# Graph kernel: late weight chunks held back and reordered, gathered source rows issued 12 tiles ahead, logits split on ScalarE

## The chip, the cores and the metric

The kernel runs on one core of one Trainium2 chip. The metric is device time in microseconds (us) of one execution; a profile shows a single execution's engines, queues and waits. Engines are named as in the profile: PE is TensorE's matmuls and PEld its weight loads, DVE is VectorE, ACT is ScalarE, POOL is GpSimd, SP is SyncE, which only issues transfers here.

## What is computed

256 nodes with 1024 features and 8448 edges (src, dst), sorted by dst.

```python
h = relu(layernorm(x))
feat = concat([h[src], h[dst]], 1)                    # 8448 x 2048
e_f = relu(feat @ W_kind + b_kind)                    # kind: hh (128 edges), oo (640), ho (the rest)
logit = (e_f @ W_a + b_a)[:, 0]
alpha = softmax of logit over the edges of each dst
z = segment_sum(alpha * h[src], dst)                  # 256 x 1024
x = x + relu(concat([h, z], 1) @ W_hn (rows 0 to 63) or W_on (the others) + b)
h = relu(layernorm(x))
x = x + h @ Wd.T + bias                               # Wd: 1024 edge weights scattered; here by 256 x 256 counts
```

## The kernel before, in words

The edges lie in 66 tiles of 128. For the oo and ho edges the product with `W_kind` is taken per node and not per edge: TensorE makes the tables P = h @ top half and Q = h @ bottom half, ScalarE stores them in HBM, and POOL gathers a tile's P rows by src into `Gp` (12 slots, `p_rows`, L308) and its Q rows by dst into `Gq` (8 slots, `q_rows`, L320), 512 KB each. The first tile (hh, tile number 0 in the code) goes through TensorE directly.

`lots()` cuts the 66 tiles into 24 lots of mostly 3. The 65 gathered tiles are counted 0 to 64 below in the order of `GATHERED`; lot 2 is the hh tile, lots 17 and 18 are oo, lot 19 holds gathered tiles 53 to 55, lot 20 56 to 58, lot 21 59 to 61, lot 22 62 and 63, lot 23 64.

- VectorE, per tile: `total` (L584) adds P and Q rows and counts `s_sum`; `onehot` (L575, L577) makes the one-hot maps of src and dst for the next lot; `logit` (L588) takes relu times `wa` with a row sum and counts `s_used`. Per lot: `lot_split` (L630, L631) adds b_a and cuts the logits into a high part `lgh` and a rest `lgl`. It stands behind the first sum of the next lot (`lot_start`). After lot 19 comes `few_max`, after lot 20 `few_sums`.
- ScalarE, per tile: the source one-hots times edge weights (`weight_products`, L414, high and low) and, when the split is through, times logits (`logit_products`, L426, high and low).
- TensorE, per lot g: first `JOBS_IN[g]` jobs, then `lot_count(g + 1)` (L809 into psB and psW), then `lot_place(g)` (L809 into psA, 12 matmuls for 3 tiles). `PACE` lists the jobs of lots 3 on. A job of the first three units is one chunk of 512 KB (L897, 16 matmuls); the last unit has eight jobs, 0 to 7, each with a pair of chunks "on" and "hn" of the top halves (L914, L919, L921). Jobs 0 and 1 stand in lot 16, jobs 2 to 5 in lots 17 to 20, and jobs 6 and 7 behind the last placing. Then come the transposes of A (L941), the products with `rows_h` (L950) and the lower halves (L955, L975, L980).
- SP loads weight chunks into the 4 slots of `W` (L227), each as soon as the job four chunks (in the last unit two jobs) before has used the slot. Behind the last of these stand, in this order, eight hn chunks (L247) and `rows_h` (L250), which go into slots of `Gp` as their last tiles are used, the last bias (L252), and x again (L254 to L257).
- POOL issues 12 P gathers, 12 Q gathers, and then Q and P of each tile in turn. Q(i) waits for the sum of tile i - 8, P(i) for the logit of tile i - 12.

After the last lot VectorE makes the softmax (L674 to L700), whose result A the transposes wait for.

The last job and its loads in `block.sync`, which say what the order is:

```python
for q in range(WSLOTS, CHUNKS):
    ...
    sp.wait_ge(s_wused, uses_before(q))
    load(q)
for k in range(KC):
    sp.wait_ge(s_used, FREED + k + 1)
    sp.dma_start(hn_w[k], ...).then_inc(s_hn, 16)
```

Here FREED is 53.

Of the kernel before, what the change touches and what calls it, by code (L numbers as in the profile page):

```python
# [4 lines left out]
P = 128  # L5
N = 256
NT = N // P
D = 1024
KC = D // P
# [8 lines left out]
LOT = 3  # L18
# [12 lines left out]
LOTS = lots()  # L31
# [4 lines left out]
ENTRY = [len(EARLY) + sum(map(len, LOTS[:g])) for g in range(NLOTS + 1)]  # L36
# [6 lines left out]
WSLOTS = 4  # L43
NP = 12
NQ = 8
# [7 lines left out]
CHUNKS = SPLIT + HH + PLAIN + 2 * KC  # L53
PACE = [2, 2, 2, 2] + [2, 2, 1, 2, 1] + [2, 2, 2, 2] + [2, 1, 1, 1, 1]
# [3 lines left out]
HN_SLOT = [(FREED + k) % NP for k in range(KC)]  # L58
ROW_SLOT = (FREED + KC) % NP
# [10 lines left out]
FREED_Q = len(GATHERED) - NQ  # L70
assert FREED_Q % NQ + 3 <= NQ
# [3 lines left out]
def uses_before(q):  # L75

    gone = q - WSLOTS
    return gone + 1 if gone < SPLIT + HH + PLAIN else SPLIT + HH + PLAIN + (gone - SPLIT - HH - PLAIN) // 2 + 1


def gnn_block(nc, x, edge_ids, edge_w, weights, bias_rows, w_a, b_a, l1_bias, out):
# [13 lines left out]
    with ctx:  # L95
# [59 lines left out]
        lgl = sb("lgl", [P, 2, LOT], f32r)  # L155
# [43 lines left out]
        s_hh, s_split = sem("hh_logit"), sem("logits_split")  # L199
# [22 lines left out]
        def _(sp):  # L222
# [14 lines left out]
            for q in range(WSLOTS, CHUNKS):  # L237
                if q - WSLOTS < SPLIT:
                    sp.wait_ge(s_lo, q - WSLOTS + 1)
                else:  # L240
                    sp.wait_ge(s_wused, uses_before(q))
                load(q)
                if q == 2 * WSLOTS:
                    sp.dma_start(wa[:, :], w_a.broadcast_to((P, D))).then_inc(s_wa, 16)
            for k in range(KC):
                sp.wait_ge(s_used, FREED + k + 1)
                sp.dma_start(hn_w[k], weights[(CHUNKS + k) * P:(CHUNKS + k + 1) * P, :]).then_inc(s_hn, 16)  # L247
            sp.wait_ge(s_used, FREED + KC + NT)
            sp.wait_ge(s_hst, 16)
            sp.dma_start(rows_h, by_tile(h_rows)).then_inc(s_hr, 16)  # L250
            sp.wait_ge(s_used, FREED + KC + NT + 1)
# [18 lines left out]
        def _(pool):  # L270
# [55 lines left out]
            for i in range(NP):  # L326
                q_rows(i)
            for i in range(NP, len(GATHERED)):
                q_rows(i)
                p_rows(i)  # L330

        @block.scalar
        def _(act):
# [83 lines left out]

            def logit_products(g):

                act.wait_ge(s_split, g + 1)  # L420
                for i, t in enumerate(LOTS[g]):
                    n = LTH[t]
                    if n >= LRING:
                        act.wait_ge(s_placed, n - LRING + 1)
                    for half, val in enumerate((lgh, lgl)):
                        last = nc.scalar.activation(RL[:, n % LRING, half, :],  # L426
                                                    ohs[:, (ENTRY[g] + i) % RING, :].bitcast(f32), ACT.Copy,
                                                    scale=val[:, g % 2, i:i + 1].bitcast(f32))
                    last.then_inc(s_lprod, 1)

            def guard_counts():

                act.wait_ge(s_counted, ET)
                act.wait_ge(s_sum, FREED_Q + 1)
                nc.scalar.activation(inv[:, :, :], psC, ACT.Relu, bias=minus[:, 0:1]).then_inc(s_cm, 1)
                nc.scalar.activation(off[:, :, :], psC, ACT.Relu, bias=unit[:, 0:1], scale=-1.0).then_inc(s_cm, 1)
                act.wait_ge(s_cm, 2)
                nc.scalar.mul(off[:, :, :], off[:, :, :], NEG).then_inc(s_cm, 1)
# [61 lines left out]
        def _(dve):  # L500
# [8 lines left out]
            def chain(ins):  # L509
                dve.wait_ge(s_v, mark(ins))  # L510
# [95 lines left out]
            def lot_logits(g):  # L606

                for k, t in enumerate(LOTS[g]):
# [12 lines left out]
            def lot_split(g):  # L621

                size = len(LOTS[g])
                if LOTS[g][0]:
                    dve.wait_ge(s_used, PLACE[LOTS[g][-1]] + 1)
                else:
                    dve.wait_ge(s_hh, 1)
                if g >= 2:
                    dve.wait_ge(s_lprod, LTH[LOTS[g - 2][-1]] + 1)
                chain(nc.vector.tensor_scalar(lgh[:, g % 2, 0:size], lg[:, g % 2, 0:size], bar[:, 0:1], None, ALU.add))  # L630
                nc.vector.scalar_tensor_tensor(out=lgl[:, g % 2, 0:size], in0=lg[:, g % 2, 0:size], scalar=bar[:, 0:1],  # L631
                                               in1=lgh[:, g % 2, 0:size].bitcast(f32), op0=ALU.add, op1=ALU.subtract
                                               ).then_inc(s_split, 1)

            def few_counts():

                dve.wait_ge(s_few, 2)
                chain(nc.vector.tensor_scalar(inv_few[:, :, :, :], few[:, :, :, :], 1.0, None, ALU.max))
                chain(nc.vector.reciprocal(inv_few[:, :, :, :], inv_few[:, :, :, :]))
                chain(nc.vector.tensor_scalar(off_few[:, :, :, :], few[:, :, :, :], 0.5, NEG, ALU.is_lt, ALU.mult))  # L640

# [21 lines left out]
            for g in range(NLOTS):  # L663
                lot_logits(g)
                lot_start(g + 1)
                lot_split(g)
# [62 lines left out]
        def _(pe):  # L729
# [149 lines left out]
            def job(j):  # L879
# [22 lines left out]
                q = SPLIT + HH + PLAIN + 2 * k  # L902
# [135 lines left out]
```

## Time and profile before

| | us |
|---|---|
| median of 3 runs | 348.86 (348.76 to 349.54) |
| the profiled execution | 349.19 |
| its span | 347.40 |
| PE busy in it | 308.9 (89%) |
| DVE busy | 262.2 (75%) |
| ACT busy | 161.3 (46%) |
| POOL busy | 162.1 (47%) |
| bytes moved by DMA | 122.06 MB, mean 351 GB/s |

The profiled execution is 0.33 us over the median; 1.79 us of it lie outside the span. Times below are us from the span's start. The share of an engine is a mean over very different stages, so the slices and windows are the place to see what is full when. Instructions that overlap in an engine's pipeline are shown with their whole durations.

### The profile page before, as it was taken

How to read it: one execution, taken by the hardware profiler on the slowest of the kernel's cores; microseconds unless marked ns; L12 is line 12 of the kernel's file. 1: busy time of each engine (PE TensorE's matmuls, PEld its weight loads, DVE VectorE, ACT ScalarE, POOL GpSimd, SP SyncE). 2: the span in 40 equal slices, each digit the busy share in tenths (PEclk: the TensorE clock that was granted, in tenths of full speed). 3: DMA queues.
4: the chain of work that ended last, by engine and by line, in shares of the span. 5: the costliest groups of instructions: out<-in, count | busy, mean ns of one | idle time of the engine just before them, and what ended most of it. 6: DMA issues, size and time to landing. Idle time of an engine off the chain costs nothing.

```text
span 347.4 us, 4106 instructions
## 1 busy us (share of the span) xinstructions
PE 308.9 (89%) x1359; PEld 198.5 (57%) x1359; DVE 262.2 (75%) x475; ACT 161.3 (46%) x345; POOL 162.1 (47%) x148
## 2 busy tenths in 40 slices
PE   0899999997999999999999999999899586549993
PEld 0687688653566665666666665566345455433632
DVE  4646448557947999999899997889966899875334
ACT  3773441642353555485435764543254454524011
POOL 3110087056433887777767885888855400000000
PEclk9999999999999999999999999999999898669996
DMA  7997879999999999999999999999999999990003
GB/s 259 355 330 281 276 292 387 406 337 413 409 409 409 402 403 411 409 408 417 411 408 410 410 412 412 409 408 411 409 409 408 408 410 411 406 350 15 0 2 121
DMA packets 34425, 122.06 MB, mean 351 GB/s; under 512 B 4058, under 2 KB 4570, under 8 KB 34404
## 3 DMA queue, kind: packets, MB, share of 16 engines
q0 software_dynamic: 19008, 69.21, 50.3%
q1 hardware_dynamic: 14004, 47.34, 36.1%
q10 hardware_dynamic: 1392, 5.24, 3.7%
q8 instruction: 11, 0.18, 0.2%
q14 instruction: 10, 0.08, 0.1%
HBM read 115.49 MB, written 6.29 MB: 351 GB/s over the span
## 4 chain that ended last, share of the span: by engine, by line
PE 49%; DMA 23%; POOL 15%; issue 6%; DVE 4%; ACT 2%; POOLq 0%; ACTq 0%
DMA Gp<-p_ho,ids 17%; PE psG L759 12%; PE psG L897 12%; POOL Gq L320 8%; POOL Gp L308 7%; DMA W<-weights 5%; PE psG L865 5%; PE psW L809 4%; PE psA L809 3%; PE psB L809 2%; PE psG L975 2%; PE psG L914 1%; PE psW L950 1%; PE psG L955 1%; DMA xs<-x 1%
## 5 line engine op out<-in xcount | busy, mean ns | idle before, releaser
L320 POOL DMA_INDIRECT Gq<-q_ho,ids x60 | 76.4, 1273 | 55.3 <-DVE Gp L584 30.8
L584 DVE TENSOR_TENSOR Gp<-Gp,Gq 128x1024 f32<-128x1024 f32 x65 | 79.2, 1219 | 23.9 <-DMA Gp<-p_ho,ids 14.8
L308 POOL DMA_INDIRECT Gp<-p_ho,ids x60 | 66.1, 1101 | 42.9 <-DMA p_ho<-T 24.9
L897 PE MATMUL psG<-W,hT 128*128 128x512 f32 x192 | 84.6, 593 | 0.0
L588 DVE SCALAR_TENSOR_TENSOR Gp<-Gp,wa 128x1024 f32<-128x1024 f32 x65 | 79.0, 1215 | 0.1
L426 ACT ACTIVATE RL<-ohs,lgh 128x256 fp32r<-128x256 f32 x66 | 32.9, 499 | 64.7 <-DVE lgl L631 64.7
L897 PEld LDWEIGHTS psG<-W,hT 128*128 128x128 f32 x192 | 35.5, 190 | 40.1 <-issue 40.1
L414 ACT ACTIVATE RW<-ohs,ewh 128x256 fp32r<-128x256 f32 x66 | 33.1, 502 | 48.1 <-DVE ohs L575 44.3
L809 PE MATMUL psA<-RL,ohd 128*128 128x256 f32 x240 | 37.8, 314 | 13.0 <-ACT RL L426 13.0
L809 PE MATMUL psW<-RW,ohd 128*128 128x256 f32 x264 | 45.6, 295 | 0.3
L809 PEld LDWEIGHTS psA<-RL,ohd 128*128 128x128 f32 x240 | 34.4, 214 | 15.9 <-ACT RL L426 14.4
L809 PEld LDWEIGHTS psW<-RW,ohd 128*128 128x128 f32 x264 | 37.0, 193 | 3.9 <-issue 2.6
L809 PE MATMUL psB<-ohs,ohd 128*128 128x256 f32 x132 | 32.6, 335 | 3.9 <-DVE ohd L577 3.9
L537 DVE TENSOR_TENSOR Wl<-W,Wh 128x1024 fp32r<-128x1024 f32 x16 | 19.6, 1223 | 21.5 <-ACT Wh L349 21.5
L414 ACT ACTIVATE RW<-ohs,ewl 128x256 fp32r<-128x256 f32 x66 | 32.6, 494 | 0.0
L426 ACT ACTIVATE RL<-ohs,lgl 128x256 fp32r<-128x256 f32 x66 | 32.5, 493 | 0.0
L865 PE MATMUL psG<-W,hsT 128*128 128x512 f32 x64 | 30.2, 602 | 2.6 <-DMA W<-weights 2.6
L809 PEld LDWEIGHTS psB<-ohs,ohd 128*128 128x128 f32 x132 | 21.5, 193 | 14.2 <-issue 7.1
L575 DVE TENSOR_SCALAR ohs<-iota,idf 128x256 fp32r<-128x256 f32 x72 | 25.6, 356 | 4.5 <-PE psA L809 4.4
L577 DVE TENSOR_SCALAR ohd<-iota,idf 128x256 fp32r<-128x256 f32 x72 | 26.4, 366 | 0.0
L349 ACT CAST Wh<-W 128x1024 fp32r<-128x1024 f32 x16 | 16.8, 1050 | 17.3 <-PE psG L759 16.4
L759 PE MATMUL psG<-Wh,hTh 128*128 128x512 f32 x64 | 21.2, 412 | 1.4 <-DVE hTl L543 1.4
(154 smaller groups left out, 334.1 us busy)
## 6 DMA issues: line engine op xcount, KB each, us to landing
W<-weights SPq DMA_DIRECT2D x72, 512.0 KB, 7.2
Gp<-weights SPq DMA_DIRECT2D x8, 512.0 KB, 14.9
xs<-x SPq DMA_DIRECT2D x2, 512.0 KB, 3.7
h_rows<-h ACTq DMA_DIRECT2D x1, 1024.0 KB, 6.0
p_ho<-T ACTq DMA_DIRECT2D x2, 512.0 KB, 4.6
q_ho<-T ACTq DMA_DIRECT2D x2, 512.0 KB, 7.2
p_oo<-T ACTq DMA_DIRECT2D x1, 1024.0 KB, 9.6
q_oo<-T ACTq DMA_DIRECT2D x1, 1024.0 KB, 11.1
```

Of the source, the lines that this page charges most:

```text
L308: nc.gpsimd.indirect_dma_start(out=Gp[:, i % NP, :], out_offset=None, in_=p_oo if t <= OO_TILES else p_ho, in_offset=bass.IndirectOffsetOn ...
L320: nc.gpsimd.indirect_dma_start(out=Gq[:, i % NQ, :], out_offset=None, in_=q_oo if t <= OO_TILES else q_ho, in_offset=bass.IndirectOffsetOn ...
L414: last = nc.scalar.activation(RW[:, w % WRING, half, :], ohs[:, (first + i) % RING, :].bitcast(f32), ACT.Copy, scale=val[:, t:t + 1].bitca ...
L426: last = nc.scalar.activation(RL[:, n % LRING, half, :], ohs[:, (ENTRY[g] + i) % RING, :].bitcast(f32), ACT.Copy, scale=val[:, g % 2, i:i ...
L575: nc.vector.tensor_scalar(ohs[:, n % RING, :], iota[:, :], idf[:, tile, 0:1], None, ALU.is_equal).then_inc(s_ohs, 1)
L577: nc.vector.tensor_scalar(ohd[:, n % RING, :], iota[:, :], idf[:, tile, 1:2], None, ALU.is_equal).then_inc(s_ohd, 1)
L584: nc.vector.tensor_tensor(Gp[:, i % NP, :], Gp[:, i % NP, :], Gq[:, i % NQ, :], ALU.add).then_inc(s_sum, 1)
L588: nc.vector.scalar_tensor_tensor(out=Gp[:, i % NP, :], in0=Gp[:, i % NP, :], scalar=0.0, in1=wa[:, :], op0=ALU.max, op1=ALU.mult, accum_ou ...
L759: ins = nc.tensor.matmul(psG[:, 2 * t + half, :], lhs[:, k, cols], rhs[:, s, half * HALF:(half + 1) * HALF], start=not opened and k == 0 a ...
L809: ins = nc.tensor.matmul(bank[:, c, :], ohd[:, slot, c * P:(c + 1) * P], m, start=False, stop=False, skip_group_check=True)
L865: last = nc.tensor.matmul(psG[:, half, :], hsT[:, c, k, :], W[:, q % WSLOTS, half * HALF:(half + 1) * HALF], start=False, stop=c == 1 and ...
L897: last = nc.tensor.matmul(psG[:, 2 * t + half, :], hT[:, k, t * P:(t + 1) * P], W[:, s, half * HALF:(half + 1) * HALF], start=u != 1 and k ...
```

## The change

- POOL: 12 P gathers, 8 Q gathers, then Q(i) and P(i + 4) in turn; at the end only Q.
- SP: the loop over chunks ends with the pair of job 4. Then: wait for 56 sums, the pair of job 5; wait for 59 sums and for 55 used tiles, `rows_h`; hn chunks 0 to 3; the pair of job 6; hn chunks 4 to 7; the pair of job 7. `rows_h` gets the slots that come free first, the hn chunks the ones behind. The bias and x stay last.
- TensorE: jobs 0 to 5 stand in lots 16, 17, 18, 20, 21 and 22; 6 and 7 stay behind the last placing.
- ScalarE makes the split: a copy of the lot's logits to `lgh` when the lot's last tile is used, then the rest per tile in an Identity with a bias, and the products, the first high product before the rests. `lot_split` goes from VectorE, together with its wait, which moves to the head of `lot_logits`.
- b_a is no longer in the logits but in the offsets (`off_few`, `off`), one VectorE operation more, early, and one ScalarE operation in another form.

```diff
-PACE = [2, 2, 2, 2] + [2, 2, 1, 2, 1] + [2, 2, 2, 2] + [2, 1, 1, 1, 1]
+PACE = [2, 2, 2, 2] + [2, 2, 1, 2, 1] + [2, 2, 2, 2] + [1, 1, 1, 0, 1, 1, 1]
...
-HN_SLOT = [(FREED + k) % NP for k in range(KC)]
-ROW_SLOT = (FREED + KC) % NP
+ROW_SLOT = FREED % NP
+HN_SLOT = [(FREED + NT + k) % NP for k in range(KC)]
...
+LATE_TOP, LATE_TILES, HN_TILES = 5, 56, 59
...
-            for q in range(WSLOTS, CHUNKS):
+            for q in range(WSLOTS, TOPS + 2 * LATE_TOP):
...
-            for k in range(KC):
-                sp.wait_ge(s_used, FREED + k + 1)
+            def load_top(k):
+                for q in range(TOPS + 2 * k, TOPS + 2 * k + 2):
+                    sp.wait_ge(s_wused, uses_before(q))
+                    load(q)
+
+            def load_hn(k):
+                sp.wait_ge(s_used, FREED + NT + k + 1)
                 sp.dma_start(hn_w[k], weights[(CHUNKS + k) * P:(CHUNKS + k + 1) * P, :]).then_inc(s_hn, 16)
-            sp.wait_ge(s_used, FREED + KC + NT)
+
+            sp.wait_ge(s_sum, LATE_TILES)
+            load_top(5)
+            sp.wait_ge(s_sum, HN_TILES)
             sp.wait_ge(s_hst, 16)
+            sp.wait_ge(s_used, FREED + NT)
             sp.dma_start(rows_h, by_tile(h_rows)).then_inc(s_hr, 16)
+            for k in range(4):
+                load_hn(k)
+            load_top(6)
+            for k in range(4, KC):
+                load_hn(k)
+            load_top(7)
...
             for i in range(NP):
                 p_rows(i)
-            for i in range(NP):
+            for i in range(NQ):
                 q_rows(i)
-            for i in range(NP, len(GATHERED)):
+            for i in range(NQ, len(GATHERED)):
                 q_rows(i)
-                p_rows(i)
+                if i - NQ + NP < len(GATHERED):
+                    p_rows(i - NQ + NP)
...
+            def logit_product(g, i, half, val):
+                n = LTH[LOTS[g][i]]
+                if half == 0 and n >= LRING:
+                    act.wait_ge(s_placed, n - LRING + 1)
+                return nc.scalar.activation(RL[:, n % LRING, half, :], ohs[:, (ENTRY[g] + i) % RING, :].bitcast(f32),
+                                            ACT.Copy, scale=val[:, g % 2, i:i + 1])
...
+                size, first = len(LOTS[g]), LTH[LOTS[g][0]]
+                if LOTS[g][0]:
+                    act.wait_ge(s_used, PLACE[LOTS[g][-1]] + 1)
+                else:
+                    act.wait_ge(s_hh, 1)
+                nc.scalar.copy(lgh[:, g % 2, 0:size], lg[:, g % 2, 0:size]).then_inc(s_lgh, 1)
+                logit_product(g, 0, 0, lg)
+                act.wait_ge(s_lgh, g + 1)
+                for i in range(size):
+                    nc.scalar.activation(lgl[:, g % 2, i:i + 1], lgh[:, g % 2, i:i + 1].bitcast(f32), ACT.Identity,
+                                         bias=lg[:, g % 2, i:i + 1], scale=-1.0).then_inc(s_lgl, 1)
+                for i in range(size):
+                    if i:
+                        logit_product(g, i, 0, lg)
+                    act.wait_ge(s_lgl, first + i + 1)
+                    logit_product(g, i, 1, lgl).then_inc(s_lprod, 1)
...
-                nc.scalar.mul(off[:, :, :], off[:, :, :], NEG).then_inc(s_cm, 1)
+                nc.scalar.activation(off[:, :, :], off[:, :, :], ACT.Identity, bias=bar[:, 0:1], scale=NEG).then_inc(s_cm, 1)
...
+                if g >= 2:
+                    dve.wait_ge(s_lprod, LTH[LOTS[g - 2][-1]] + 1)
...
-            def lot_split(g):
...
+                chain(nc.vector.tensor_scalar(off_few[:, :, :, :], off_few[:, :, :, :], bar[:, 0:1], None, ALU.add))
...
                 lot_start(g + 1)
-                lot_split(g)
```

## Rows read from the trace of the kernel before

**Rows 1.** The page's slices of 8.7 us: DMA share in tenths and GB/s.

```profile
DMA  7997879999999999999999999999999999990003
GB/s 259 355 330 281 276 292 387 406 337 413 409 409 409 402 403 411 409 408 417 411 408 410 410 412 412 409 408 411 409 409 408 408 410 411 406 350 15 0 2 121
```

**Rows 2.** Windows: busy time of each engine, granted clock, DMA share and rate.

```profile
core 0: us, PE busy (x) PEld busy (x) DVE busy (x) ACT busy (x) POOL busy (x), PEclk, DMA share, GB/s
110.00:240.00 130.00, 130.00 (x590) 83.52 (x589) 122.32 (x233) 72.30 (x169) 101.22 (x82) 1.00 1.03 409
240.00:270.00 30.00, 27.55 (x125) 13.49 (x124) 21.69 (x42) 11.40 (x27) 19.01 (x16) 1.00 1.03 409
...
290.00:300.00 10.00, 6.26 (x27) 5.30 (x27) 9.80 (x19) 4.31 (x12) 0.00 (x0) 0.67 1.03 410
...
306.00:312.00 6.00, 3.45 (x13) 3.06 (x14) 5.86 (x9) 2.55 (x6) 0.00 (x0) 0.53 0.94 347
312.00:320.00 8.00, 8.00 (x27) 2.60 (x26) 5.30 (x19) 2.96 (x6) 0.00 (x0) 0.93 0.08 31
```

**Rows 3.** Queues (packets, MB, share) in 240:270 twice, 260:270, 280:290, 300:306 twice.

```profile
q0 software_dynamic: 2091, 7.61, 63.7%
q1 hardware_dynamic: 1262, 4.65, 38.8%
...
q1 hardware_dynamic: 542, 2.02, 50.5%
...
q1 hardware_dynamic: 210, 0.79, 19.9%
...
q1 hardware_dynamic: 637, 2.34, 97.9%
q0 software_dynamic: 29, 0.10, 4.1%
```

**Rows 4.** VectorE's timeline from tile 55's sum on: start, duration, instruction, wait.

```profile
269.81 1.23 DVE L584 TENSOR_TENSOR Gp<-Gp,Gq 128x1024 f32<-128x1024 f32 x1 [3.16 <-DMA Gp<-p_ho,ids]
...
273.49 1.22 DVE L584 TENSOR_TENSOR Gp<-Gp,Gq 128x1024 f32<-128x1024 f32 x1 [0.79 <-DMA Gp<-p_ho,ids]
274.64 0.22 DVE L630 TENSOR_SCALAR lgh<-lg,bar 128x3 fp32r<-128x3 f32 x1
...
300.86 1.23 DVE L584 TENSOR_TENSOR Gp<-Gp,Gq 128x1024 f32<-128x1024 f32 x1 [1.02 <-DMA Gp<-p_ho,ids]
...
305.94 1.23 DVE L584 TENSOR_TENSOR Gp<-Gp,Gq 128x1024 f32<-128x1024 f32 x1 [2.59 <-DMA Gp<-p_ho,ids]
...
308.62 0.08 DVE L588 DVE_READ_ACCUMULATOR Gp<-Gp,wa 128x1 f32 x1
...
309.12 0.42 DVE L674 TENSOR_SCALAR inv<-inv 128x512 f32<-128x512 f32 x1
...
317.44 0.62 DVE L700 TENSOR_SCALAR A<-A,den 128x256 f32<-128x256 f32 x2
```

**Rows 5.** TensorE's timeline: starts of jobs 3, 4, 5, last placing, job 6, transposes.

```profile
258.04 1.88 PE L914 MATMUL psG<-W,hT 128*128 128x512 f32 x4
...
264.90 1.88 PE L914 MATMUL psG<-W,hT 128*128 128x512 f32 x4
...
278.90 1.93 PE L914 MATMUL psG<-W,hT 128*128 128x512 f32 x4
...
308.55 2.93 PE L809 MATMUL psA<-RL,ohd 128*128 128x256 f32 x12 [5.93 <-ACT RL L426]
311.28 2.80 PE L914 MATMUL psG<-W,hT 128*128 128x512 f32 x4
...
319.66 0.66 PE L941 MATMUL psB<-ident,A 128*128 128x128 f32 x4
```

**Rows 6.** ScalarE's timeline: the last low product and a one-column operation with bias.

```profile
309.65 0.49 ACT L426 ACTIVATE RL<-ohs,lgl 128x256 fp32r<-128x256 f32 x1
...
329.84 0.29 ACT L491 ACTIVATE sd<-mv,epst 128x1 f32<-128x1 f32 x1 [4.60 <-DVE mv L712]
```

**Rows 7.** Transfers: W chunks and hn chunks (landing times), SP's issue of hn.

```profile
W<-weights SPq DMA_DIRECT2D x72, 512.0 KB, 7.2
...
DMA to landing us min/median/max: 11.0/14.9/17.4
...
283.59 11.12 SPq L247 DMA_DIRECT2D Gp<-weights  x8
```

More of the change, by code:

```diff
@@ L52 @@
 JOBS = 4 * KC
-CHUNKS = SPLIT + HH + PLAIN + 2 * KC
-PACE = [2, 2, 2, 2] + [2, 2, 1, 2, 1] + [2, 2, 2, 2] + [2, 1, 1, 1, 1]
+TOPS = SPLIT + HH + PLAIN
+CHUNKS = TOPS + 2 * KC
+PACE = [2, 2, 2, 2] + [2, 2, 1, 2, 1] + [2, 2, 2, 2] + [1, 1, 1, 0, 1, 1, 1]
 JOBS_IN = [0] * (HH_LOT + 1) + PACE + [0] * (NLOTS - HH_LOT - 1 - len(PACE))
 FREED = len(GATHERED) - NP
-HN_SLOT = [(FREED + k) % NP for k in range(KC)]
-ROW_SLOT = (FREED + KC) % NP
+ROW_SLOT = FREED % NP
+HN_SLOT = [(FREED + NT + k) % NP for k in range(KC)]
 BREP_SLOT = (FREED + KC + NT) % NP
@@ L77, in uses_before @@
     gone = q - WSLOTS
-    return gone + 1 if gone < SPLIT + HH + PLAIN else SPLIT + HH + PLAIN + (gone - SPLIT - HH - PLAIN) // 2 + 1
+    return gone + 1 if gone < TOPS else TOPS + (gone - TOPS) // 2 + 1
 def gnn_block(nc, x, edge_ids, edge_w, weights, bias_rows, w_a, b_a, l1_bias, out):
@@ L154, in gnn_block @@
         lgh = sb("lgh", [P, 2, LOT], f32r)
-        lgl = sb("lgl", [P, 2, LOT], f32r)
+        lgl = sb("lgl", [P, 2, LOT], f32)
         brow, ew = shared(("brow", [LOW0 + 32, D], f32), ("ew", [P, ET], f32))
@@ L198, in gnn_block @@
         s_ewh, s_bh, s_bl = sem("weights_high"), sem("biases_high"), sem("biases_low")
-        s_hh, s_split = sem("hh_logit"), sem("logits_split")
+        s_hh, s_lgh, s_lgl = sem("hh_logit"), sem("logits_high"), sem("logits_low")
         s_ohs, s_ohd = sem("src_onehot"), sem("dst_onehot")
@@ L416, in weight_products @@
                     last.then_inc(s_wprod, 1)
-            def logit_products(g):
[L420 to L429, printed above, removed]
+            def logit_product(g, i, half, val):
[4 more added lines that the diff above has]
+                                            ACT.Copy, scale=val[:, g % 2, i:i + 1])
+            def logit_products(g):
+                size, first = len(LOTS[g]), LTH[LOTS[g][0]]
[14 more added lines that the diff above has]
+                    logit_product(g, i, 1, lgl).then_inc(s_lprod, 1)
             def guard_counts():
@@ L619, in lot_logits @@
                         hh_logit(col)
-            def lot_split(g):
[L623 to L633, printed above, removed]
             def few_counts():
@@ L901, in job @@
                     return
-                q = SPLIT + HH + PLAIN + 2 * k
+                q = TOPS + 2 * k
                 on, hn = q % WSLOTS, (q + 1) % WSLOTS
```

## The prediction

> **What bounds the kernel now.** I read the page's slices first: from about 61 us (slice 8) to 304 us (slice 35) the DMA engines are full and move some 410 GB/s, and from 313 us to the end they are idle [rows 1]. The windows say what else is full. Between 110 and 240 us TensorE has no idle time, VectorE is busy 122.3 of 130 us, and DMA is at its limit too. After 240 us only DMA stays full: VectorE works 21.7 of 30 us [rows 2]. So the kernel has a transfer-bound body and a tail of dependences. Under a full DMA the order of the bytes is what counts: whatever lands before the last gathered rows delays them, unless VectorE is late anyway.
>
> The DMA queues say who took the bytes [rows 3]. Between 240 and 270 us the gathers (q0) got 7.61 MB and SP's queue (q1) 4.65 MB, and in the last ten of these us q1 had as much as q0. I number the gathered tiles 0 to 64 and the eight pairs of "top" chunks (L910 to L923) 0 to 7. VectorE's timeline [rows 4] shows the effect. Tile 55 is summed at 269.81 us, after a wait of 3.16 us for its rows. From there VectorE is nearly continuous: to tile 64 at 305.94 us there are 36.13 us, of which only 0.79 + 1.02 + 2.59 = 4.40 us are waits. So two things set the last sum: when tile 55's rows land, and VectorE's own work behind it.
>
> From the last sum the end hangs by a chain: logit, split, products on ScalarE, placing on TensorE, softmax on VectorE; beside it TensorE does pairs 6 and 7 from 311.28 us, and the transposes of L941 start at 319.66 [rows 5], although A was ready at 317.44 + 0.62 = 318.06 us [rows 4]. The last sum to the transposes is 13.72 us; behind them nothing of the change acts, 27.74 us to the end of the span.
>
> **The change part by part.**
>
> *Source rows 12 ahead.* P rows were issued with the Q rows of the same tile; now Q(i) is followed by P(i+4). No gather is added. Q(i) then has 3 more half tiles of 0.524 MB ahead of it in the queue (P(i+1) to P(i+3); before, P(i) came last): 1.57 MB, while the queue is full. At 409 GB/s that is 3.8 us later for every tile up to about 60. For tile 64 nothing is ahead that was not there before. Not shown in the trace is how many landed rows lie ready before 240 us. Bounds: 0, if the buffers are full then, and 1.57 MB / 0.205 = 7.7 us, if q1 holds its half share all the time. I take 3.8: VectorE waits for rows in this stretch, so the buffers are empty. POOL now waits for the logit of tile i-8 before a P row; the Q row queued behind that waits for the next sum, which starts as the logit ends, 1.2 us later, so the P issue hides in it.
>
> *Tops spread and held.* A pair's load needs the slot of two jobs earlier. Before, jobs 3, 4 and 5 start at 258.04, 264.90 and 278.90 us [rows 5] and take 3.8 to 4.2 us; so pair 5 was fetched when job 3 was through (about 262 us) and pair 6 behind job 4, at 269. Now two jobs move out of lots 16 and 19: job 3 follows the placing of lot 19, which needs tile 55's logit. The wait for 56 sums comes before that and is empty. So pair 5 (1.05 MB) is no longer fetched before tile 55: -1.05 / 0.409 = -2.6 us. Pair 6 mostly landed behind tile 55 before, too; I count nothing for it there.
> Tile 55: 269.81 + 3.8 - 2.6 = 271.1 us (bounds 267.2 and 274.9).
>
> *Split on ScalarE.* VectorE loses L630 and L631. In lot 19's case they take it from 274.64 to 275.10; I count 1.25 us for the splits of lots 19, 20 and 21, and (309.12 - 308.70) 0.42 for the one behind the last logit, with as much for the one between tile 64's sum and its logit [rows 4]. From tile 55 to tile 64: 36.13 - 4.40 - 1.25 = 30.5 us if no rows are late. Last sum: 271.1 + 30.5 = **301.6 us**, 4.3 earlier.
> ScalarE gets a copy and up to three one-column operations per lot. The nearest row is the one-column operation with a bias, 0.29 us [rows 6]; bounds 0.1 (its pipelined spacing) and 0.3. At 4 x 0.29 = 1.2 us in a lot of 8.5 us or more, ScalarE, idle half of the time, hides it; if it were full, this would come on every placing. In the last lot the chain from the logit's end (308.62 + 0.08 us) to the products was 309.65 + 0.49 - 308.70 = 1.44 us [rows 6] and becomes 0.25 + 0.45 + 0.25 + 0.49 = 1.44: no change.
> The products of lot 22 no longer wait for tile 64's sum (the split stood behind it), so only one tile instead of three is left to place after the last logit, 0.5 instead of 2.93 us.
> The b_a that leaves the logits is added to the offsets: 0.7 us on VectorE near 74 us, before its 6 us wait for the first Q rows; L438 keeps its price. Both zero; if tile 0's rows came earlier, 0.7.
>
> *TensorE behind the last sum.* Tile 64's logit ends 2.4 us after 301.6, products at 305.4, placed at 305.9. Pairs 6 and 7 took 8.2 us, from the end of the placing (308.55 + 2.93 = 311.48) to 319.66 [rows 5], so the transposes can start at 314.1. Part of the 8.2 is a slow clock (four matmuls of job 6 took 2.80 us, the same four of job 5 1.93); I leave it in. VectorE: 304.0 + 8.94 (309.12 to 318.06) = 312.9, not later. Transposes 5.5 us earlier.
>
> *Held loads.* Job 3 ends near 283.3 us (tile 55's logit 273.9, products 276.9, placing to 279.5, job 3.8). Then SP issues pair 5, rows_h (59 sums: 284.7), hn 0 to 3, pair 6 (after job 4, about 295), hn 4 to 7, pair 7 (after job 5, about 303.8), the bias, x. SP's order puts the hn chunks 4 to 7 behind pair 6; they are needed only 8 us after the transposes. Pair 7: 303.8 + 7.2, the median landing of a W chunk [rows 7], = 311.0, and the second chunk 0.6 later; job 7's second half then ends at 313.5. Just covered; if not, every us goes into the end. From 300 us on 2.34 MB [rows 3] + 6 x 0.347 + 8 x 0.031 = 4.7 MB moved before [rows 2]; with about 8 MB behind the last gather now, 8 / 0.409 = 20 us from 293 ends at 313, before x and the bias are used (about 320).
> *A page against it.* At 283 us I have 7.87 MB - 12 x 0.409 = 3.0 MB of gathers left. In 280:290 q1 got 19.9% [rows 3] although its loads were issued from 283.59 us on [rows 7]; at that share the rest needs 9 us, plus the 5.9 us by which the last rows lagged (0.10 MB in 300:306): 298, hidden. The Trainium skill (DMA: Bandwidth & Descriptors, Queues, rings and completion order) says that each DMA engine takes turns between the queues that have work, packet by packet, so loads let loose at 283 would take half. By row 260:270 this is so, by 280:290 not. With a half share the rest needs 14.6 us: 303.5, 1.9 us late, and the sum is 1.9 worse.
>
> **Sum.** Last sum -4.3, the way from it to the transposes -1.2 (13.72 to 12.5): -5.5 us. The profiled execution has 347.40 us of span and 1.79 around it, 349.19 us, 0.33 over the median of the runs. 349.19 - 5.5 = 343.7, against the median **343.4 us**.
>
> **The rivals.**
> 1. *Rows ahead cost nothing* (buffers filled before). Tile 55 at 267.2, last sum 297.7, transposes 310.2 by TensorE. But the bytes still end at 313, and x and the bias (1.57 MB, 3.8 us) come behind pair 7, so it lands at 309 to 310 and the transposes come at 312: -7.7, 341.2; without that floor 339.4. For: VectorE shows 122.3 busy us of 130 from 110 to 240 us [rows 2], so rows were mostly there. Against: VectorE's waits after 240. 17%.
> 2. *Half share for the held loads*, as above: 345.3. 8%.
> 3. *TensorE's clock.* The granted clock averages 0.67 in 290:300 and 0.53 in 306:312 [rows 2], where TensorE waits between lots; twelve placings take 2.93 us at the lower level (1.2 GHz). Now job 5 stands before the last two placings. At 1.2 GHz it takes 7.6 instead of 3.8 us: last placing about 309, transposes about 317.3: 346.5. Against: jobs 3 to 5 in lots 20 to 22 make TensorE busier. 11%. The Trainium skill (TensorE: Matmul & The Clock Gate, Part 1) has the same two levels, the lower after idling; the trace agrees.
> 4. *Slower: pair 7 is late.* It waits in SP's order behind hn 7 and for job 5. hn chunks took up to 17.4 us to land [rows 7]. 303.8 + 17.4 = 321.2, + 1.9 = 323.1 against 319.66: +3.4, 352.3. It decides from a landing at 317.8. Against: gathers are over by then and DMA has about 3 MB left. 10%.
> 5. *It does not hold.* The two waits on sums are empty or nearly; if the jobs' order brings nothing either, the time is 348.9. 5%.
>
> The forecast (341.5 to 345.5) has 49%. Range **339.8 to 347.5 us**: rival 1, 2 and most of 3 inside, 4 and 5 outside. Faster by over 0.2% (what a measurement of this kernel can tell) 0.85, within 0.05, slower 0.10.
>
> **What would show it.** Right: tile 55 summed near 271 us, with waits between tiles 40 and 55 larger than before; no wait above 0.5 us from tile 56 on; q1 nearly empty in 271:283 us; last sum near 302; transposes at 314, released by the pairs, not by W. Wrong: tile 55 beyond 275 (rows ahead dearer), L919 waiting for W at the end (rival 4), a clock near 0.5 in 295:310 (rival 3), waits for Q rows at tiles 60 to 64 (rival 2).

## The result and the profile after

The changed kernel took 343.10 us in the median of 5 runs (340.22 to 343.81), the kernel before 348.76 us beside it (5 runs, 346.62 to 349.54). The ratio is 0.9865, with a 95% interval of 0.9823 to 0.9906. Forecast were 343.4 us and a range of 339.8 to 347.5. Here and below the ratio and its interval leave out the few executions that fell into a slower state of the chip (one of six in e4 and in e6, one of the kernel before beside e5 to e8 and one beside e12), while the medians count them.

The profiled execution of after is the fastest of its five: 340.22 us with a span of 338.4, against 349.19 and 347.40 before. So 3 of the 9 us between the two profiles belong to these executions and not to the change. To read the rest I set a zero where both kernels still run the same code: the start of TensorE's first job of one chunk (L897 before, L918 after), at 110.30 us before and 107.03 after. "From zero" below means from that start. It shows what the medians show: the transposes of A come 209.36 us from zero before and 203.64 after, 5.7 us less.

The page's slices of after (DMA share in tenths, then GB/s), to be held against [rows 1]:

```profile
DMA  7989879999999999999999999999999999997003
GB/s 277 336 313 326 307 280 414 390 336 406 410 408 410 410 407 409 410 408 417 410 409 410 409 411 414 409 410 408 409 411 408 408 409 408 409 405 269 2 0 124
```

No byte went away (122.06 MB in both). The transfer-bound body is as full as it was; what changed is who moves in it. (The last slice, with 124 GB/s, and 121 before, is the output: the prediction's "idle to the end" holds up to it.) The windows of after (columns as in [rows 2]):

```profile
110.00:240.00 130.00, 130.00 (x588) 83.18 (x586) 111.38 (x195) 79.26 (x216) 93.38 (x79) 1.00 1.03 410
240.00:270.00 30.00, 21.07 (x100) 12.94 (x101) 26.12 (x45) 14.27 (x42) 19.82 (x17) 0.91 1.03 409
270.00:280.00 10.00, 8.65 (x35) 5.32 (x34) 8.86 (x14) 7.10 (x17) 1.68 (x1) 0.76 1.03 410
280.00:290.00 10.00, 6.98 (x30) 4.87 (x30) 9.93 (x18) 5.47 (x16) 0.00 (x0) 0.83 1.03 408
290.00:300.00 10.00, 8.58 (x47) 5.05 (x48) 9.76 (x15) 7.58 (x22) 0.00 (x0) 1.00 1.03 409
306.00:312.00 6.00, 5.48 (x23) 1.81 (x20) 3.35 (x16) 3.61 (x8) 0.00 (x0) 1.00 0.84 285
```

Between 240 and 270 us VectorE is now busy 26.12 us instead of 21.69: rows come faster there. The lost time stands earlier, 111.38 busy us in 110:240 instead of 122.32. In part that is the split that left VectorE; the rest is waiting for rows, 12.2 us in that window instead of 4.9. From 290 us on TensorE's granted clock is 1.00, where it was 0.67 and 0.53; in 240:270 and 270:280 it is lower than before, 0.91 and 0.76 against 1.00 and 0.83.

The queues of after in 240:270, 270:280 and 280:290, q0 and q1 each (packets, MB, share; before in [rows 3]):

```profile
q0 software_dynamic: 2501, 9.11, 76.1%
q1 hardware_dynamic: 860, 3.14, 26.3%
...
q0 software_dynamic: 1126, 4.09, 102.6%
q1 hardware_dynamic: 4, 0.01, 0.2%
...
q0 software_dynamic: 600, 2.18, 54.8%
q1 hardware_dynamic: 496, 1.88, 47.4%
```

The gathers (q0) got 9.11 MB instead of 7.61, then had the engines alone for ten us. SyncE's timeline of after says when it let go of the rest:

```profile
260.94 18.18 SPq L230 DMA_DIRECT2D W<-weights  x4
281.82 0.39 SPq L263 DMA_DIRECT2D Gp<-h_rows  x1
...
291.92 0.81 SPq L230 DMA_DIRECT2D W<-weights  x2
292.77 3.92 SPq L256 DMA_DIRECT2D Gp<-weights  x4
301.49 0.80 SPq L230 DMA_DIRECT2D W<-weights  x2
```

The x4 from 260.94 are the pairs 4 and 5 (the latter at 278.32). 291.92 is pair 6, and the last two lines are hn 4 to 7 and pair 7. VectorE's timeline of after, the lines that answer to [rows 4] (tiles 55, 56, 63, 64, the last logit, A):

```profile
266.89 1.23 DVE L617 TENSOR_TENSOR Gp<-Gp,Gq 128x1024 f32<-128x1024 f32 x1 [0.34 <-DMA Gq<-q_ho,ids]
...
271.04 1.23 DVE L617 TENSOR_TENSOR Gp<-Gp,Gq 128x1024 f32<-128x1024 f32 x1 [1.25 <-DMA Gq<-q_ho,ids]
...
296.26 1.22 DVE L617 TENSOR_TENSOR Gp<-Gp,Gq 128x1024 f32<-128x1024 f32 x1
...
298.66 1.22 DVE L617 TENSOR_TENSOR Gp<-Gp,Gq 128x1024 f32<-128x1024 f32 x1
...
301.14 0.42 DVE L695 TENSOR_SCALAR inv<-inv 128x512 f32<-128x512 f32 x1
...
309.45 0.62 DVE L721 TENSOR_SCALAR A<-A,den 128x256 f32<-128x256 f32 x2
```

Behind tile 56 no sum waits for rows any more, where 63 and 64 waited 1.02 and 2.59 us. The rows waited for are now `Gq`, since the P rows run ahead. TensorE's timeline of after (job 5, last placing, jobs 6 and 7, transposes; before in [rows 5]):

```profile
297.69 1.88 PE L935 MATMUL psG<-W,hT 128*128 128x512 f32 x4
...
301.37 2.01 PE L830 MATMUL psA<-RL,ohd 128*128 128x256 f32 x12
303.21 1.88 PE L935 MATMUL psG<-W,hT 128*128 128x512 f32 x4
...
306.89 1.98 PE L935 MATMUL psG<-W,hT 128*128 128x512 f32 x4
...
310.67 0.66 PE L962 MATMUL psB<-ident,A 128*128 128x128 f32 x4
```

The last placing follows job 5 without the wait of 5.93 us, and jobs 6 and 7 follow each other to the transposes.

### The profile page after: what moved, and what is told of

It reads as the page before. It is cut to its first block, busy times and chain, and to the rows that moved or that the text cites. A ratio compares the mean times of both kernels' runs of the same rounds, so it can differ in the third digit from the quotient of the medians.

```text
span 338.4 us, 4122 instructions
## 1 busy us (share of the span) xinstructions
PE 306.0 (90%) x1354; PEld 195.9 (58%) x1359; DVE 254.0 (75%) x428; ACT 177.1 (52%) x435; POOL 159.4 (47%) x148
## 2 busy tenths in 40 slices
DMA packets 34425, 122.06 MB, mean 361 GB/s; under 512 B 4058, under 2 KB 4570, under 8 KB 34404
## 4 chain that ended last, share of the span: by engine, by line
PE 42%; DMA 29%; DVE 15%; POOL 6%; issue 4%; ACT 3%; another core or an unknown queue 1%; ACTq 0%; DVEq 0%
DMA Gq<-q_ho,ids 23%; PE psG L780 12%; PE psG L918 8%; PE psG L886 5%; DVE Gp L617 5%; DMA W<-weights 5%; DVE Gp L621 4%; POOL Gq L339 3%; PE psW L830 3%; POOL Gp L327 3%; PE psA L830 2%; PE psG L996 2%; PE psB L830 2%; PE psW L971 1%; PE psG L935 1%
## 5 line engine op out<-in xcount | busy, mean ns | idle before, releaser
L339 POOL DMA_INDIRECT Gq<-q_ho,ids x60 | 72.9, 1215 | 48.5 <-DVE Gp L617 22.7
L327 POOL DMA_INDIRECT Gp<-p_ho,ids x60 | 68.3, 1138 | 49.2 <-DMA p_ho<-T 24.9
L918 PE MATMUL psG<-W,hT 128*128 128x512 f32 x192 | 84.6, 592 | 0.0
L918 PEld LDWEIGHTS psG<-W,hT 128*128 128x128 f32 x192 | 35.4, 190 | 40.1 <-issue 40.1
L830 PE MATMUL psA<-RL,ohd 128*128 128x256 f32 x240 | 36.7, 302 | 6.6 <-ACT RL L442 6.3
L830 PEld LDWEIGHTS psA<-RL,ohd 128*128 128x128 f32 x240 | 32.5, 202 | 11.0 <-ACT RL L442 10.0
L442 ACT ACTIVATE RL<-ohs,lg 128x256 fp32r<-128x256 f32 x66 | 32.8, 497 | 0.0
L610 DVE TENSOR_SCALAR ohd<-iota,idf 128x256 fp32r<-128x256 f32 x72 | 25.7, 357 | 0.0
L780 PE MATMUL psG<-Wh,hTh 128*128 128x512 f32 x64 | 20.5, 402 | 1.4 <-DVE hTl L576 1.4
## 6 DMA issues: line engine op xcount, KB each, us to landing
q_oo<-T ACTq DMA_DIRECT2D x1, 1024.0 KB, 11.4
```

The source lines that it names most:

```text
L327: nc.gpsimd.indirect_dma_start(out=Gp[:, i % NP, :], out_offset=None, in_=p_oo if t <= OO_TILES else p_ho, in_offset=bass.IndirectOffsetOn ...
L339: nc.gpsimd.indirect_dma_start(out=Gq[:, i % NQ, :], out_offset=None, in_=q_oo if t <= OO_TILES else q_ho, in_offset=bass.IndirectOffsetOn ...
L442: return nc.scalar.activation(RL[:, n % LRING, half, :], ohs[:, (ENTRY[g] + i) % RING, :].bitcast(f32), ACT.Copy, scale=val[:, g % 2, i:i ...
L610: nc.vector.tensor_scalar(ohd[:, n % RING, :], iota[:, :], idf[:, tile, 1:2], None, ALU.is_equal).then_inc(s_ohd, 1)
L780: ins = nc.tensor.matmul(psG[:, 2 * t + half, :], lhs[:, k, cols], rhs[:, s, half * HALF:(half + 1) * HALF], start=not opened and k == 0 a ...
L830: ins = nc.tensor.matmul(bank[:, c, :], ohd[:, slot, c * P:(c + 1) * P], m, start=False, stop=False, skip_group_check=True)
```

## The experiments

Each was run beside the kernel before on the same chip, whose median was 347.33 us for e1 to e4, 347.48 for e5 to e8, 347.39 for e9 to e11 and 347.15 for e12. The expectations are quoted as they were on record before each run.

**e1: the split alone.**

```diff
 # the changed kernel, with PACE, SyncE's order and POOL's order of before
-PACE = ... + [1, 1, 1, 0, 1, 1, 1]
+PACE = ... + [2, 1, 1, 1, 1]
```

> Of the change only the split on ScalarE (with b_a in the offsets). Theory A (the order of the bytes decides, VectorE's splits count only behind tile 55): the last rows still land near 306 us, so only the way from the last sum to the transposes gets shorter, 13.7 to 12.5 us: about 347.6 us. Theory B (VectorE's work is what was too long, each of 24 splits counts about 0.4 us): the last sum comes 2 us or more earlier, 344 to 345 us.

349.39 us, ratio 1.0056 (1.0022 to 1.0090): slower than either theory had it.

**e2: source rows ahead alone.**

```diff
 # the kernel before, with POOL's order of after
-            for i in range(NP):
+            for i in range(NQ):
                 q_rows(i)
```

> Of the change only the P rows 12 tiles ahead. Theory A: tile 55 is summed 3.8 us later (273.6 instead of 269.8), no row wait behind it, last sum 273.6 + 31.7 = 305.3 instead of 305.9: 348.2 us, no difference that can be told. Rival (rows ahead cost nothing and take the last waits away): last sum 301.5, 344.5 us.

349.31 us, ratio 1.0045 (1.0016 to 1.0073). Tile 55 was summed at 273.69 us and the last tile at 305.26, both as theory A had them; the time is about 2 us over the kernel before, which it had not.

**e3: the hold alone.**

```diff
 # the kernel before, with PACE and SyncE's order of after
-PACE = ... + [2, 1, 1, 1, 1]
+PACE = ... + [1, 1, 1, 0, 1, 1, 1]
```

> Of the change only the jobs' order (PACE) and SP's order with its two waits. Theory A: tile 55 at 269.8 - 2.6 = 267.2, no row wait behind it, last sum 298.9; the transposes wait for job 7, whose pair lands at 309 to 310, so about 312 instead of 319.7: 341.8 us, as fast as the whole change or faster. Theory B (the parts only work together): 345 us or more.

343.23 us, ratio 0.9874 (0.9830 to 0.9918), 1.4 us more than theory A.

**e4: the changed kernel without rows ahead.**

```diff
-            for i in range(NQ):
+            for i in range(NP):
                 q_rows(i)
```

> The changed kernel with POOL's order as before (P and Q of the same tile). Theory A: tile 55 at 267.2, last sum 297.7, transposes at 312 by the landing of pair 7: 341.2 us, 2 us faster than the whole change. Rival (rows ahead help, or at least fill a gap): 345 us, slower than the whole change.

342.49 us, ratio 0.9836 (0.9783 to 0.9889), between theory A and the rival: not 2 us faster than the whole change.

So the gain is all in the hold, each of the two other parts alone is about half a per cent slower, and rows ahead, dropped from the whole, changed nothing clear, although they cost 3.9 us at tile 55 when alone. TensorE's timeline at job 7, first e3:

```profile
308.25 3.32 PE L931 MATMUL psG<-W,hT 128*128 128x512 f32 x4 [2.35 <-DMA W<-weights]
```

then e4:

```profile
307.70 2.66 PE L934 MATMUL psG<-W,hT 128*128 128x512 f32 x4 [3.67 <-DMA W<-weights]
```

Both wait for pair 7, and in both the four matmuls behind the wait run slower than the 1.98 us they take in after; the granted clock in 306:312 is 0.73 in e3 and 0.74 in e4, 1.00 in after. From there to the transposes both need 5.43 us, after 3.78. VectorE was done earlier (last sum at 295.73 us in e4), and pair 7's landing took its place as the end. That calls for pair 7 sooner.

**e5: the changed kernel again**, no edit, beside e6 to e8.

> The changed kernel unaltered, beside the others of this call. Both theories: 1.2 to 1.8% under before. Tile 55 near 267 to 271 us, last sum 298.7 to 302, job 7 without a wait for W, transposes 12.0 to 12.5 us behind the last sum.

342.61 us, ratio 0.9896 (0.9851 to 0.9941). Job 7 waited 0.17 us for `W`.

**e6: pair 7 ahead of hn 4 to 7**, without rows ahead.

```diff
             load_top(6)
+            load_top(7)
             for k in range(4, KC):
                 load_hn(k)
-            load_top(7)
```

> POOL's order as before (no rows ahead), the rest of the change, and pair 7 loaded ahead of hn chunks 4 to 7. Theory A (without rows ahead the transposes wait only for pair 7, which stands behind 2.1 MB of hn chunks that are needed 8 us later): issued at 298.5 behind nothing but pair 6, landed near 306, job 7 without a wait, transposes near 308.5 instead of 313.1: about 4.5 us faster than the run without rows ahead, some 338 us. Rival (the wait moves: hn chunks 4 to 7, now issued after 298.5, and the bias and x land too late): the last products wait for them, 341 to 343 us, no gain.

338.24 us, ratio 0.9746 (0.9699 to 0.9794): faster than both kernels. Against e4, which differs only in pair 7's place, the two intervals just touch, and the profiles have the transposes 5.9 us earlier. SyncE's timeline of e6 (pairs 6 and 7, then hn 4 to 7) and the end of TensorE's:

```profile
290.06 9.67 SPq L230 DMA_DIRECT2D W<-weights  x4
299.77 1.92 SPq L256 DMA_DIRECT2D Gp<-weights  x4
```

```profile
301.29 1.88 PE L934 MATMUL psG<-W,hT 128*128 128x512 f32 x4
...
304.97 1.98 PE L934 MATMUL psG<-W,hT 128*128 128x512 f32 x4
...
308.75 0.66 PE L961 MATMUL psB<-ident,A 128*128 128x128 f32 x4
```

The second half of the x4 is pair 7, through at 299.73 us; hn 4 to 7 follow. Job 7 waits for nothing, and the hn chunks still come in time: the products that use them start at 317.13 us without a wait.

**e7: the changed kernel without its two waits on sums.**

```diff
-            sp.wait_ge(s_sum, LATE_TILES)
             load_top(5)
-            sp.wait_ge(s_sum, HN_TILES)
```

> The changed kernel without its two waits on sums (56 before pair 5, 59 before rows_h). Theory A (the slots and the jobs' order hold the loads back, the waits are empty, the second worth 2 us of SP's time): pair 5 at the same time, rows_h 2 us earlier, the same time as the whole change within 0.3%. Theory B (the waits do the holding): last sum later by up to 2.6 us, 345 to 346 us.

341.79 us, ratio 0.9863 (0.9814 to 0.9911): no difference from e5 that can be told. In the changed kernel the waits hold back next to nothing: only `rows_h` had stood 2.2 us for its sums in after, and that without effect on the time.

**e8: the jobs' order alone.**

```diff
-PACE = ... + [2, 1, 1, 1, 1]
+PACE = ... + [1, 1, 1, 0, 1, 1, 1]
```

> Of the change only the jobs' order (PACE); SP's order as before. Theory A: tile 55 and the last sum come as early as with the whole hold (298 to 299 us), and pair 7 lands earlier, but the hn chunks and rows_h stand behind pair 7, issued only after job 5 (about 301 us), so rows_h lands near 317 and the product behind the transposes (L950) waits for it: 346 to 349 us, the gain is given back. Rival (SP's order does not matter): 342 to 343 us.

354.30 us, ratio 1.0228 (1.0181 to 1.0275), outside what was expected. The transposes are early, 201.71 us from zero; the time is lost behind them. TensorE's timeline of e8:

```profile
311.49 0.65 PE L941 MATMUL psB<-ident,A 128*128 128x128 f32 x4
320.94 7.06 PE L950 MATMUL psW<-AT,Gp 128*128 128x64 f32 x32 [8.79 <-DMA Gp<-h_rows]
```

SyncE's of e8 (pairs 5 to 7, then the hn chunks and `rows_h`):

```profile
281.37 22.06 SPq L227 DMA_DIRECT2D W<-weights  x6
303.48 4.38 SPq L247 DMA_DIRECT2D Gp<-weights  x8
307.98 0.39 SPq L250 DMA_DIRECT2D Gp<-h_rows  x1
```

and the windows of e8:

```profile
290.00:300.00 10.00, 8.33 (x44) 4.98 (x43) 9.93 (x17) 6.04 (x13) 0.00 (x0) 1.00 0.33 124
...
320.00:330.00 10.00, 9.06 (x35) 8.00 (x36) 0.00 (x0) 0.58 (x1) 0.00 (x0) 0.50 0.42 145
```

SyncE stands at pair 7, whose slot job 5 holds, and behind it stand 5.2 MB, of which the 4.2 MB of hn chunks could have gone as their slots came free: DMA moves 124 GB/s for ten us. They go at 303 to 308 us, too late, and after 8.79 us of idling TensorE takes 7.06 us for the 32 products that took 3.79 in after, at a granted clock of 0.50.

**e9: SyncE's order alone**, with its two waits.

```diff
 # the kernel before, PACE unchanged
+            sp.wait_ge(s_sum, LATE_TILES)
+            load_top(5)
+            sp.wait_ge(s_sum, HN_TILES)
...
```

> The kernel before with SyncE's new order alone (two sum waits, rows_h first, hn chunks in two fours, pairs 6 and 7 in between); the jobs stay in lots 16 to 20. Theory (the hold needs both halves: the jobs' order keeps pair 5 and its followers from being fetched early, SyncE's order keeps the queue free behind it): here job 5 is still through by lot 20, so pairs 6 and 7 and the hn chunks are issued from about 276 to 290 us and meet the last 4 MB of gathers. At half a share those last 4 / 0.205 = 19 us, to 295, so the last sum is at about 300 instead of 305.9, and all eight jobs' chunks are there in time: transposes at 314, time 343 to 345. In that case the sum wait at 56 is NOT empty: it holds pair 5 back by several us. Rival (the jobs' order is the half that counts, SyncE's order only makes it harmless): rows of the late tiles come no earlier than before, last sum 304 to 306, time 346.5 to 348.

342.94 us, ratio 0.9886 (0.9850 to 0.9922): in time as much as the whole hold. What SyncE waited for in e9, 255:300 us (total, times, longest):

```profile
SPq L261 <- DVE Gp L601: 11.4, 1, 11.4
...
SPq L229 <- DVE Gp L601: 7.7, 1, 7.7
```

With the jobs in their old lots the waits on sums are far from empty: `rows_h` (L261) stood 11.4 us, pair 5 (L229) 7.7 us.

At the last sum e9 gives less than the jobs' order alone (191.23 us from zero, e8 189.34, e3 with both 189.36). It isn't behind in time because pair 7 was issued early enough for job 7 to wait for nothing. And the jobs in their old lots leave TensorE's clock low towards the end, as before; e9's window, to be held against 1.00 in e3, e8 and after:

```profile
290.00:300.00 10.00, 4.62 (x18) 3.86 (x18) 8.18 (x14) 5.19 (x11) 0.00 (x0) 0.58 1.03 408
```

**e12: SyncE's order without the two waits**.

```diff
 # e9
-            sp.wait_ge(s_sum, LATE_TILES)
             load_top(5)
-            sp.wait_ge(s_sum, HN_TILES)
```

> SyncE's new order alone as in e9, but without its two waits on sums. In e9 those waits held pair 5 back by 7.7 us and rows_h by 11.4 us. Theory (with the jobs in their old lots it is the waits that hold): pair 5 is issued at about 259 and is fetched ahead of tile 55's rows again, 1.05 / 0.409 = 2.6 us, rows_h and hn 0 follow at 267 to 271 and take a half share; from job 0 to the last sum 194 to 195.5 us instead of 191.2 (before: 195.6), time 345.5 to 347. Rival (the order of SyncE's queue alone does it, since the hn chunks and pair 6 cannot start before their slots come free anyway): 191 to 192 us from job 0 to the last sum, time 342.5 to 343.5, as e9.

349.88 us, ratio 1.0071 (1.0046 to 1.0095), above both expectations. The waits are worth about 7 us here. SyncE's `rows_h` went at 266.64 us instead of 279.70, and VectorE's last sums waited again:

```profile
303.25 1.23 DVE L599 TENSOR_TENSOR Gp<-Gp,Gq 128x1024 f32<-128x1024 f32 x1 [2.29 <-DMA Gp<-p_ho,ids]
...
308.37 1.23 DVE L599 TENSOR_TENSOR Gp<-Gp,Gq 128x1024 f32<-128x1024 f32 x1 [2.63 <-DMA Gp<-p_ho,ids]
```

The last sum came 198.21 us from zero, 3 us later than the theory had it and 2.6 later than in the kernel before. A likely cause, which no run took apart: `rows_h`, issued last in the kernel before, and the first hn chunks (from 272.27 us instead of 283.59) now go earlier, and SyncE's queue moved 1.61 MB in 270:280 instead of 1.12.

**e10: e6 with rows ahead.**

```diff
 # e6
-            for i in range(NP):
+            for i in range(NQ):
                 q_rows(i)
```

> The changed kernel whole, with the source rows 12 ahead kept, and pair 7 loaded ahead of hn chunks 4 to 7. Theory (rows ahead cost about 3.5 us at tile 55 and the last sum, and in the changed kernel this is hidden because pair 7's landing sets the end; with pair 7 early nothing hides it): last sum near 299.5, transposes 12.0 behind it at 311.5, so 2.5 to 3 us slower than the same kernel without rows ahead (338.24): 341 us, hardly better than the changed kernel (342.6). Rival (what the variant without rows ahead gained comes from pair 7's place alone): 338 to 339 us, transposes at 309.

342.19 us, ratio 0.9862 (0.9827 to 0.9896). With rows ahead, pair 7's new place brings nothing; without them it brings some 4 us. e10 and e6 ran beside different runs of the kernel before, but the intervals of the two ratios are apart.

**e11: e6 with the split on VectorE.**

```diff
 # the kernel before, with PACE and SyncE's order of e6
```

> The kernel before with the held loads and the jobs' new order alone, pair 7 ahead of hn chunks 4 to 7; the split stays on VectorE. Theory (the split takes 1.25 us from VectorE between tiles 55 and 64 and orders the last placings; with the end set by the last sum it counts in full): last sum 1.2 to 2 us later than with the split on ScalarE, transposes at 309.5 to 311, time 339.5 to 340.5 against 338.24. Rival (the split brings nothing, as it brought nothing alone): 338.0 to 338.6.

340.27 us, ratio 0.9808 (0.9759 to 0.9857), against 0.9746 with the split on ScalarE. The intervals overlap a little; the profiles (below) have the last sum 1.8 us and the transposes 2.1 us later. So the split most likely helps once nothing else sets the end, but the times alone don't prove it.

The milestones, us from zero, worked out from the timelines of one profiled execution each:

| | tile 55 | last sum | transposes | last sum to transposes |
|---|---|---|---|---|
| before | 159.51 | 195.64 | 209.36 | 13.72 |
| after | 159.86 | 191.63 | 203.64 | 12.01 |
| e5 after again | 160.07 | 191.54 | 203.79 | 12.25 |
| e7 no sum waits | 159.52 | 190.58 | 203.33 | 12.75 |
| e10 pair 7 first, rows ahead | 159.98 | 191.54 | 203.55 | 12.01 |
| e1 split | 159.14 | 196.73 | 210.77 | 14.04 |
| e2 rows ahead | 163.46 | 195.03 | 208.14 | 13.11 |
| e3 hold | 156.85 | 189.36 | 205.79 | 16.43 |
| e11 e3, pair 7 first | 157.19 | 189.68 | 202.05 | 12.37 |
| e4 hold, split | 157.70 | 188.40 | 205.80 | 17.40 |
| e6 e4, pair 7 first | 156.84 | 187.89 | 199.91 | 12.02 |
| e8 jobs' order | 157.93 | 189.34 | 201.71 | 12.37 |
| e9 SyncE's order | 157.98 | 191.23 | 204.54 | 13.31 |
| e12 e9, no sum waits | 159.19 | 198.21 | 211.46 | 13.25 |

Up to the last sum, after, e5, e7 and e10 do nearly the same, so do e3 and e11, and e4 and e6. Each set agrees within 1.1 us, so a difference of 2 us can be read here, and one of half a us can't.

## Why the prediction was right, point by point

**The sum.** Forecast were -4.3 us at the last sum and -1.2 behind it. From zero it was -4.0 (e5: -4.1) and -1.7 (-1.5). By parts, taken off in this order, with the means of the sets, at the last sum: the hold 189.52 - 195.64 = -6.1 (forecast -2.6 at tile 55 and the -4.40 of waits behind it, -7.0); the split 188.15 - 189.52 = -1.4 (forecast -1.25); rows ahead 191.32 - 188.15 = +3.2 (forecast +3.8). Taken in this order, the terms had the right sign and about the right size. Alone, on the kernel before, they do not add up so: rows ahead gave -0.6 us at the last sum (e2), since the waits behind tile 55 went with them, and the split +1.1 (e1).

**Tile 55.** Right by its two terms, less right as a clock time. Rows ahead alone gave +3.95 (forecast +3.8), the hold alone -2.5 (forecast -2.6); together, with the split, +0.01 to +0.56 in the four profiles of that set instead of +1.2. The forecast 271.1 us was 266.89 in the profile, 3.3 us of it the earlier execution. The byte account in the full queue (1.57 MB and 1.05 MB at 409 GB/s) was the right tool there. Rival 1, rows ahead at no cost, is refuted at tile 55 and the last sum.

**From tile 55 to 64.** Forecast 30.5 us without waits; 31.77 with one wait of 1.25 us, that is 30.52. The waits of tiles 63 and 64 are gone. The one that stayed is tile 56's; with 1.25 us it is over the 0.5 us that I had set as the limit from tile 56 on.

**Where the waits would be.** Wrong: I wanted larger waits between tiles 40 and 55. They sum to 8.6 us in after and 11.0 before; the larger ones are in 110:240 (12.2 against 4.9 us). The delay of the rows was there before 240 us (tile 48 at 243.18 us, or 6.0 us later from zero than before; 4.6 in e2) and was largely made good by tile 55, as 1.5 MB fewer of SyncE's loads came in between (q1 3.14 instead of 4.65 MB). My sum had both terms at tile 55, where their net is small, and not where each acts. (The size at tile 48 is rough: e4 and e6, alike up to there, differ by 3 us at it.)

**The split's cost on ScalarE.** The one-column operation took 0.28 us (forecast 0.29), three of them 0.65, that is 0.185 us from one to the next; the lower bound of 0.1 was too low. ScalarE hid it. In the last lot the first placing no longer stood behind the last sum, as forecast: 2.01 us for 12 matmuls, begun while the last tile's products were being made.

**Behind the last sum.** Forecast 12.5 us, measured 12.01 and 12.25. The term that was a little off: pairs 6 and 7, from job 6's start to the transposes, took 8.38 us before and were left so; in after they took 310.67 - 303.21 = 7.46, since job 6 ran at the full clock (1.88 us instead of 2.80). So rival 3 was wrong in its sign: the granted clock in 290:300 is 1.00 in after, e3, e4, e6 and e8, which share the jobs' order (0.87 in e7), and 0.58 and 0.66 in e9 and e1, which have the old one. A was ready at 310.07, 0.6 us before the transposes, so both chains now end nearly together.

**Held loads and pair 7.** Forecast issues were 283.3 (pair 5), 284.7 (`rows_h`), 295 (pair 6) and 303.8 (pair 7); they came at 278.3, 281.8, 291.9 and 301.5, 2.3 to 5 us earlier, of which the earlier execution accounts for some 3. "Just covered" was exact: job 7 waited 0 us in after, 0.17 in e5, 0.66 in e7. Its place is that of the bytes and not of the issue: job 7 starts 199.6 to 200.4 us from zero in after, e3, e4, e5 and e7, although its pair was issued anywhere from 191.2 (e4) to 194.5 us (after). What I didn't draw from it: a landing that is just covered is a floor. I had it as a floor in rival 1 alone, and in the forecast not as a price of the order in which pair 7 stands last. e4 and e6 show it: the 3.2 us that rows ahead cost in the changed kernel are hidden under that floor (without rows ahead the time is the same, 342.49 us in e4 and 342.61 in e5, though the last sum is 3 us earlier; in the profiles e4's transposes are even 2.0 us behind e5's, because the wait for pair 7 also lowers the clock), and with pair 7 early they cost in full (199.91 and 203.55). Rival 4 (pair 7 late by 3.4 us) did not come, but e3 and e4, with waits of 2.35 and 3.67 us, show its mechanism as soon as VectorE is earlier.

**Half share.** In 280:290 q1 took 47.4% of the time with 496 packets against 600, as soon as SyncE had loads to issue. The Trainium skill (DMA: Bandwidth & Descriptors, Queues, rings and completion order) says the engines take turns between queues, packet by packet; this row agrees, and the 19.9% of before [rows 3] was a queue with little to do for part of the window. Asked in steps of 2 us, q1 moved nothing from 280 to 286 us there, since its loads were only issued from 283.59 us, and then took 48.2 and 51.6%. So the mechanism of rival 2 was real and my share of a fifth wrong, which was the price of reading a mean over a window in which the queue was empty at first, but its price was not paid: at 280 us only 2.29 MB of gathers were left (2.18 and 0.11 MB), not 3.0 at 283, because q0 had got 1.5 MB more before, and VectorE, busy 9.93 of 10 us, was behind its rows.

**"It does not hold".** Both waits on sums are empty or nearly, as I said (e7). But they are empty only because the jobs' order delays the same loads, as a pair's slot comes free later. The two are two locks on one door: with the jobs in their old lots the waits do nearly all of the work (e12 1.0071, e9 0.9886; e9's last sum is 1.9 us behind e3's), and without the waits the jobs' order does it (e7, and up to the last sum e8). What it needs beside it is SyncE's order, or the queue idles behind pair 7 (e8). The prediction took the hold as one thing and did not see this.

**Left open.** Why e1 and e2 are half a per cent slower than before. In e1 the last sum is 1.1 us later from zero, and job 6's first four matmuls took 3.46 us behind two short placings; whether the two belong together no run took apart. The trace shows that in e1 the last rows were late: tiles 62, 63 and 64 waited 1.00, 2.54 and 2.63 us for them, against 0, 1.02 and 2.59 before. In e2 the profiled execution has the transposes earlier than before, so the median's loss isn't in it. e9 and after reach the same time; whether the jobs' order adds anything to e6 wasn't tried.

## What to carry to other kernels

Under a full DMA, count bytes, not instructions. Each MB put ahead of the rows that the critical engine waits for costs 2.4 us at 409 GB/s. Each that is put behind them gives it back, until one of the transfers put behind becomes the one that the end waits for. When a change hides a cost under such a floor, look for the floor first: moving one pair of loads ahead of four that were needed later was worth 4 us without rows ahead and nothing with them, and only so could it be seen that this part of the change cost 3.6 us. SyncE issues its loads in the order of the program, so a load whose slot comes late must not stand ahead of loads that could go (e8). And before a queue's share is read from a window, see whether the queue had work in all of it.

## What the runs showed of the hardware

One kernel's executions differ by 1 to 3 us before the job that I took as zero, a part in which the change is hardly at work: its start lay at 107.03 to 110.30 us, and at 107.33 and 108.84 in e4 and e6, which are alike up to there. In the profile of after the first pairs of matmuls of TensorE's first large stage (L759 before, L780 after) took 0.73 and 0.62 us, where the first three took 1.22, 1.05 and 1.05 before, and the stage ended at 61.69 us instead of 62.93. The rest came between that and the zero. Behind the zero, kernels that are alike agree within 1.1 us at tile 55 and at the last sum. Two profiles should not be laid side by side by their clock times alone.

An idle wait cost TensorE twice. Behind the 8.79 us in e8 its granted clock was 0.50, and the 32 products took 7.06 us instead of 3.79. The Trainium skill (TensorE: Matmul & The Clock Gate, Part 1) has the lower level of 1.2 GHz for an engine that has idled, and the rows agree.
